# A four-layer graph network on one core: graph matrices kept as 64x64 squares instead of block-diagonal 128x128 tiles, node counts and row sums moved from TensorE to VectorE

## The reference, cut to what matters

```
L0: 8-head attention inside a graph; weights = 0.33*(softmax + adj + exp(-adj)); @ v @ W_out
L1: deg = sum(adj, -1);  agg = (adj / max(deg, eps)) @ x;  relu([x, agg] @ W.T)
L2: H = (adj != 0); w = adj[0, :];  Dn_c = 1 / sum_e H[c,e] w[e];  Be_e = 1 / sum_c H[c,e]
    conv(x, W) = Dn * (H @ (Be * (H.T @ (x @ W.T)))) + b      (1/0 is taken as 0)
    conv(layer_norm(relu(conv(x, W1))), W2) + x
L3: xg = x * sigmoid(deg * Wd + bd);  QK = sigmoid(xg @ Wqk.T + b);  s = (QK @ QK.T) * adj
    attn = s / (sum(s, -1) + eps);  relu(attn @ xg @ Wl.T + bl + xg @ Wr.T)
```

## Time and profile before

| | |
|---|---|
| timed runs, median (range) | 1393.59 us (1392.63 to 1394.86) |
| profiled execution, span from first to last instruction | 1392.5 us |
| PE busy / weight load | 1263.1 us (91%) / 1088.0 us (78%) |
| DVE / ACT / POOL busy | 962.2 us (69%) / 568.9 us (41%) / 505.1 us (36%) |
| mean granted TensorE clock | 0.979 |

### The profile page before, as it was taken

How to read it: one execution, slowest core, us unless ns; L and a number is a source line. 1 busy time by engine, 2 the same in 40 slices (tenths; PEclk the granted TensorE clock), 3 DMA queues, 4 the chain that set the end, 5 groups by cost and what they waited for, 6 DMA issues and landing times.

```text
span 1392.5 us, 30787 instructions
## 1 busy us (share of the span) xinstructions
PE 1263.1 (91%) x11784; PEld 1088.0 (78%) x11784; DVE 962.2 (69%) x2116; ACT 568.9 (41%) x1090; POOL 505.1 (36%) x632
## 2 busy tenths in 40 slices
PE   6789999999999999999999999999999999999776
PEld 4577888788788878878787888778878887888665
DVE  4787766777766677776767776677776667777553
ACT  2354353444435344353434435344443534444121
POOL 2335252442525244262423425243352524435130
PEclk9899999999999999999999999999999999999886
DMA  6000101000010100101010010101001010010000
GB/s 194 20 20 21 35 1 39 15 26 27 19 34 0 38 15 19 34 2 51 0 38 15 19 34 0 38 15 38 15 19 34 0 38 19 0 35 2 20 0 16
DMA packets 43873, 34.93 MB, mean 25 GB/s; under 512 B 19319, under 2 KB 38717, under 8 KB 43838
## 3 DMA queue, kind: packets, MB, share of 16 engines
q1 hardware_dynamic: 43112, 34.04, 7.8%
q10 hardware_dynamic: 726, 0.40, 0.2%
HBM read 26.05 MB, written 8.39 MB: 25 GB/s over the span
## 4 chain that ended last, share of the span: by engine, by line
PE 67%; DVE 20%; issue 8%; ACT 2%; POOL 1%; DMA 1%; DVEq 0%; SPq 0%; POOLq 0%; ACTq 0%
PE bank L879 16%; PE bank L881 15%; PE bank L880 15%; PE bank L1054 5%; DVE x L674 4%; PE bank L998 3%; PE bank L971 3%; DVE stats L663 3%; PE bank L875 2%; PE bank L1112 2%; DVE x L810 1%; DVE yw L821 1%; PE bank L946 1%; DVE hT_lo L604 1%; DVE dsafe L758 1%
## 5 line engine op out<-in xcount | busy, mean ns | idle before, releaser
L407 POOL TENSOR_SCALAR var<-mv 128x2 f32<-128x2 f32 (+1 forms) x192 | 48.0, 250 | 697.3 <-DVE mv L667 697.3
L499 ACT ACTIVATE hT_hi<-bank 128x512 fp32r<-128x512 f32 x160 | 89.6, 599 | 171.0 <-PE bank L998 144.4
L674 DVE TENSOR_SCALAR x<-x,mv,rstd 128x256 f32<-128x256 f32 x256 | 129.6, 553 | 30.0 <-POOL rstd L410 29.9
L410 POOL TENSOR_TENSOR rstd<-var,negh 128x2 f32<-128x2 f32 (+1 forms) x192 | 127.0, 662 | 16.0
L604 DVE TENSOR_TENSOR hT_lo<-bank,hT_hi 128x512 fp32r<-128x512 f32 x160 | 103.7, 683 | 35.3 <-ACT hT_hi L499 30.9
L511 ACT ACTIVATE v<-bank 64x256 f32<-64x256 f32 x256 | 96.8, 378 | 56.6 <-PE bank L881 53.5
L663 DVE BATCH_NORM_STATS2 stats<-x 128x6 f32<-128x256 f32 x256 | 96.4, 418 | 4.4
L516 ACT ACTIVATE prob<-prob 128x512 f32<-128x512 f32 x64 | 40.5, 633 | 127.3 <-DVE prob L708 127.3
L499 ACT ACTIVATE qT<-bank 128x512 f32<-128x512 f32 x64 | 38.3, 598 | 129.0 <-PE bank L881 129.0
L452 POOL TENSOR_TENSOR prob<-prob,srec 128x512 f32<-128x512 f32 x64 | 66.8, 1044 | 52.9 <-DVE srec L716 52.9
L457 POOL TENSOR_TENSOR prob<-prob,mix 128x512 f32<-128x512 f32 x64 | 82.2, 1284 | 6.1 <-POOL prob L452 2.1
(11 more groups left out here) (204 smaller groups left out, 3978.2 us busy)
## 6 DMA issues: line engine op xcount, KB each, us to landing
xTin<-in_x_t SPq DMA_DIRECT2D x32, 256.0 KB, 2.8
xin<-in_x SPq DMA_DIRECT2D x16, 512.0 KB, 3.7
out_x<-x SPq DMA_DIRECT2D x32, 256.0 KB, 2.3
adjA<-in_adj SPq DMA_DIRECT2D x16, 128.0 KB, 2.6
adjB<-in_adj SPq DMA_DIRECT2D x32, 64.0 KB, 3.1
r<-in_wqkv SPq DMA_DIRECT2D x2, 512.0 KB, 8.7
x<-in_wqkv SPq DMA_DIRECT2D x1, 512.0 KB, 10.4
x<-in_w_out SPq DMA_DIRECT2D x1, 512.0 KB, 10.6
```

Of the source, the lines that this page charges most:

```text
L410: pool.tensor_tensor(rstd[layer][:, lo:hi], var[layer][:, lo:hi], negh[:, lo:hi], ALU.pow).then_inc(SEM[f"rstd{n}"], 1)
L499: act.activation(dst, src[:, :], func, **kw).then_inc(SEM[ready], 1)
L674: ins = dve.tensor_scalar(x[:, t, :], x[:, t, :], mv[layer][:, t, 0:1], rstd[layer][:, t:t + 1], ALU.subtract, ALU.mult)
```

## The change

All matrices of a graph become [128, 4, 64]: partitions 0 to 63 hold the square of one graph of the tile, 64 to 127 that of the other. DVE, POOL and ACT work on 256 elements per partition where they worked on 512. On PE

- a gather is 16 matmuls of a 64x128 stationary and a 64x64 moving tile in place of 8 of 128x128; the two graphs of a tile go to two banks, so that one call fills both, at the place of the first (`agg` 0), and nothing is left for the second on PE. ACT and DVE then read a bank as one graph half (strided writes), and the next product waits for both low parts before its first chunk that needs them;
- `sim` is 16 matmuls of 128 rows and 64 columns, `graph_c` 8 of 64x64, `hyper` 4 of 64x64 with 256 moving columns per call (and its two bias matmuls as before);
- the turns `graph_m`, `graph_d` and `turn_s` are 8 matmuls each against a 64x64 identity (two passes) in place of 4 transposes (one pass);
- the turn of `edge` and the count matmuls are gone. A transposed adjacency comes from DRAM (`adj_t`, one DMA of 128 KB per group), adj's first row is spread over 64 partitions by DMA (`wrow`, two DMAs), and DVE makes the turned edges, the count and the weighted row sum.

With `ht` and `cnt` no longer in `FILLS`, the banks of stream B move on: `turn1` 0 now waits for `out3` 1 of the round before to be read (before: for `agg3` 1), `turn1` 1 for `agg3` 0. The core of the diff:

```
-FILLS = {"graph_a": ["ht"], "graph_b": ["cnt"], "graph_c": ["sym"], "graph_m": ["meanT"], "graph_d": ["gT"],
+FILLS = {"graph_a": [], "graph_b": [], "graph_c": ["sym"], "graph_m": ["meanT"], "graph_d": ["gT"],
...
+        adjB = sb("adjB", [P, T, N])
+        adjBt = sb("adjBt", [P, T, N])
+        wrow = sb("wrow", [P, T, N])
+        edgew = sb("edgew", [P, T, N])
...
+        def by_half(ap, h):
+            return ap.rearrange("p c (t h n) -> p h c t n", t=T, h=2)[:, h]
...
+                    sp.wait_ge(*count("dsum", b, 1, 1))
+                    sp.wait_ge(*count("ht_ready", b, 1, 1))
+                    sp.dma_start(adjBt[:, :, :], adj_tg[b]).then_inc(SEM["adjBt_in"], 16)
+                    for h in range(2):
+                        sp.dma_start(wrow[h * N:(h + 1) * N, :, :], adj_w[b, h, 0:1, :, :]
+                                     .broadcast_to([N, T, N])).then_inc(SEM["wrow_in"], 16)
                     sp.wait_ge(*count("meanA_ready", b, 1, 1))
                     sp.wait_ge(*count("sim_ready", b, 1, 1))
+                    sp.dma_start(adjB[:, :, :], adj_g[b]).then_inc(SEM["adjB_in"], 16)
...
+            def halves_out(g, fill, i, dst, ready):
+                act.wait_ge(*filled(fill, i, g))
+                act.activation(by_half(dst, i), bank_of(fill, i)[:, :].rearrange("p (c t n) -> p c t n", c=C, t=T),
+                               ACT.Copy).then_inc(SEM[ready], 1)
+            def low_half(pair, fill, name):
+                def part_of(g, i):
+                    dve.wait_ge(*count(f"{name}_hi", g, i + 1))
+                    dve.tensor_tensor(by_half(pair[1], i), bank_of(fill, i)[:, :].rearrange("p (c t n) -> p c t n", c=C, t=T),
+                                      by_half(pair[0].bitcast(F32), i), ALU.subtract).then_inc(SEM[f"{name}_lo"], 1)
...
+            def flipped(name, g, src):
+                pe.wait_ge(*emptied(name, 0, g))
+                dst = bank_of(name, 0)
+                for t in range(T):
+                    for h in range(2):
+                        ins = pe.matmul(dst[square(h), t * N:(t + 1) * N], src[square(h), t, :],
+                                        ident[square(h), square(h)], start=True, stop=True, skip_group_check=True)
...
+            def gathered(name, g, src, mat, halves=None):
+                for c in range(C):
+                    for t in range(T):
+                        at = slice((c * T + t) * N, (c * T + t + 1) * N)
+                        for h in range(2):
+                            if c == 0 and t == 0:
+                                pe.wait_ge(*emptied(name, h, g))
+                            ins[h] = pe.matmul(bank_of(name, h)[:, at], src[square(h), t, c * P:(c + 1) * P],
+                                               mat[square(h), t, :], start=True, stop=True, skip_group_check=True)
...
-                                 [count("spread_lo", g, c + 1) for c in range(C)]), "up", i)
+                                 [count("spread_lo", g, 2)] * C), "up", i)
```

More of the change, by code:

```diff
@@ L210, in graph_layers @@
         xg = yw
-        sim = hT0
+        pair_s, sim, sT = two("sim")
         smat = sim
-        sT = bhT
+        lend = sb("lend", [P, HID + D + P])
         simsum = sb("simsum", [P, T])
@@ L1068, in mean @@
                           + [(tile_of(aggT, c, t), chunk(wm, C + c)) for c in range(C)],
-                          ready=[count("agg_lo", g, c + 1) for c in range(C)])
+                          ready=[count("agg_lo", g, 2)] * C)
             def spread(g, i):
-                pe.wait_ge(*count("gT_ready", g, 1))
-                gathered("spread", g, i, xl[1], gT, "x2_ready")
+                if i == 0:
+                    pe.wait_ge(*count("gT_ready", g, 1))
+                    gathered("spread", g, xl[1], gT, "x2_ready")
             def up(g, i):
@@ L1108, in simi @@
                 dst = bank_of("sim", 0)
+                apart(pe, g)
                 for t in range(T):
                     for c in range(C):
-                        tile = qkT[:, c, t * P:(t + 1) * P]
-                        ins = pe.matmul(dst[:, t * P:(t + 1) * P], tile, tile, start=(c == 0), stop=(c == C - 1))
+                        for h in range(2):
+                            one = qkT[:, c, t * P + h * N:t * P + (h + 1) * N]
+                            ins = pe.matmul(dst[square(h), t * N:(t + 1) * N], one, one, start=(c == 0),
+                                            stop=(c == C - 1), skip_group_check=True)
                 now_full(ins, "sim", 0)
@@ L1130, in out3 @@
                           + [(tile_of(agg3, c, t), chunk(wlr, c)) for c in range(C)], (HID + D, HID + 2 * D),
-                          [count("agg3_lo", g, c + 1) for c in range(C)])
+                          [count("agg3_lo", g, 2)] * C)
             steps = {
@@ L1136, in _ @@
                 "turn1": lambda g, i: turned("turn1", g, i, xl[0], "x1_ready", 2),
-                "graph_a": graph_a, "graph_b": graph_b, "graph_m": graph_m, "graph_c": graph_c, "graph_d": graph_d, "agg": agg,
+                "graph_m": graph_m, "graph_c": graph_c, "graph_d": graph_d, "agg": agg,
                 "mean": mean, "spread": spread, "up": up,
```

231 lines of the change are left out of this document (95 added, 136 removed).

## The result

The changed kernel takes 1422.69 us (median of 4 runs, 1421.14 to 1423.83) against 1393.11 (4 runs, 1388.42 to 1394.86) for the kernel before on the same chip: a ratio of 1.0219, interval 1.02 to 1.0238. I had forecast 1388. It is 30 us slower, outside my range and on the other side.

What follows compares the result with a forecast made beforehand. Repeated rounds bound the kernel, their head by the chain DVE, POOL, DVE rather than PE's work. Savings of 1.5 + 2.0 + 1.4 = 4.9 us from the profiled 1392.5, with the median 1.1 above, gave 1388; range 1368 to 1397.

Steps and rivals of the forecast that it cites:

- From the end of out3 to mixmat the round runs on the chain DVE, POOL, DVE: Head of each round: claimed that DVE and POOL, not PE's work, bound it; `mixmat` to come 0.94 us earlier.
- That costs nothing as long as DVE's chain is later: `turn1` waits some 0.93 us for DVE's `out3` read under the new bank order; claimed hidden, cost 0.
- The head, 0.94: From `graph_a` to `mixmat`: halved elementwise work on DVE and POOL was to bring `mixmat` 0.94 us earlier.
- From mixmat to up: Costlier `graph_d` and waiting for both low parts leave 0.10 of 0.94 us: 1.5 us over 15 rounds.
- The sim stage, -0.14: `sim` 0.62 us less, `turn_s` and `agg3` 0.24 more each: 0.14 less a round, 2.0 us over 14 rounds.
- for going in and out: 0.23 us per group of tiled PE passes for entering and leaving tiles, taken from `pv`.
- Once: Outside the repeated round: 1.4 us saved by dropping the split of adj's rows; last two rounds 0, new DMAs nothing.
- Low clock: Rival: PE's waits and half-idle array lower its clock in most rounds, 1 to 1.5 us each: +15, 1403; chance 0.05.
- The gather streams: Rival: row tiles hide the gathers' weight loads, `agg3` takes 1.08 us, the kernel 1370; chance 0.27.

## Why the prediction was wrong, step by step

By the ratios, times 1392, the 30.5 us are: 13.5 for the loop (0.0221 less 0.0124), 4.3 for the bank order (0.9998 less 0.9967), 11.6 for the squares (0.9959 less 0.9876) and 1.1, which is not told from nothing, for moving the counts once the squares are there. The intervals leave the four uncertain by some 4, 2.5, 3 and 2 us. The split of the first two depends on the order: with the old banks first it is 1.5 for the banks and 16.3 for the loop.

A round in the written-out kernels, by the rows shown above, with `sim` by its starts on PE's timeline (705.92 and 786.99, 711.36 and 792.79; us):

| from | to | before | changed, old banks | difference | forecast |
|---|---|---|---|---|---|
| `sim` | DVE's last `out3` read | 16.03 | 16.14 | +0.11 | -0.14 |
| that read | `mixmat` | 10.93 | 10.00 | -0.93 | -0.94 |
| `mixmat` | `up` 0 | 15.45 | 16.34 | +0.89 | +0.84 |
| `up` 0 | next `sim` | 38.66 | 38.95 | +0.29 | 0 |
| the round | | 81.07 | 81.43 | +0.36 | -0.24 |

So in a round the stretch with `hyper` and the `sim` stage failed, by 0.29 and 0.25; the two largest terms came as forecast. (The sum of the working, 1393.6 less 4.9, is 1388.7; it was put down as 1388.)

**"From the end of out3 to mixmat the round runs on the chain DVE, POOL, DVE" and the loop's length.** Wrong by omission, and the largest part. Nothing in my working asked how many instructions PE's loop holds. The trace had it: 24 instruction packets for the whole kernel before, so the loop was not refetched, and 104 matmuls with 104 loads added to each round (13448 less 11784, by 16). The runs with idle matmuls show that length brings the refetch and the gap. What I can't settle is the size in the changed kernel: the 13.5 us hold the refetch and whatever else differs between the two kernels' loops. In the profiled executions a round without a stretch of low clock took 83.40 us in the loop and 81.87 written out, before 82.26 and 81.07: 1.53 and 1.19, which is 4 us in 13 rounds. The five rounds of the loop that have such a stretch are together 7 us longer than the others, and the same kernel written out has none. So about half of this share goes with the clock. Whether the stall brings the clock down no run shows; with 200 idle instructions the stall is there in 12 rounds and only two have such a stretch.

**"That costs nothing as long as DVE's chain is later" (the bank wait).** Wrong. I compared PE's arrival at `graph_m` with `meanA` and found slack. But DVE stands in its own order behind `turn1`: the low halves come before `deg`, so `turn1`, ACT's copy and DVE's low half head the very chain that I took as later. Written out it costs 4.3 us (a round is 81.87 with the new banks, 81.44 with the old). In the loop it seems to hide in the gap behind the jump, which would be why restoring the banks there gave nothing that can be told.

**The head, 0.94.** Right: 0.93 from DVE's last `out3` read to `mixmat`. (From `sim` to `mixmat` it is only 0.72 by the chain's rows, because that stretch holds the `sim` stage too.) But the cause is the squares, not the counts. With the squares alone the same stretch takes 9.95 us (726.52 to 736.47), `mixmat` no longer waits at all (in the kernel before written out it waits 0.73), and PE waits 0.89 for `edge`. On PE the counts lay in slack, on VectorE they are on the chain, and only at 256 elements does this come out even.

**"From mixmat to up", 0.10 left.** Right in the sum, by luck: 0.04 is left (0.93 less 0.89). PE waits for the second low part as forecast (0.22 at `up` 0; 4.8 us over 16 in the looped kernel), and `graph_d` cost next to nothing where I had 0.24; but the product of `mean` has become 0.3 slower. First pass of it and first pass of `v`, before written out and squares alone:

```profile
735.08 0.37 PE L879 MATMUL bank<-wm_hi,hT_hi 128*128 128x256 f32 x1
...
740.62 0.40 PE L879 MATMUL bank<-wv_hi,xT_hi 128*128 128x512 f32 x1
```

```profile
738.88 0.38 PE L888 MATMUL bank<-wm_hi,hT_hi 128*128 128x256 f32 x1
...
744.73 0.39 PE L888 MATMUL bank<-wv_hi,xT_hi 128*128 128x512 f32 x1
```

5.54 us against 5.85 for the same 48 passes, and 5.86 with the counts moved as well. It isn't the banks (both have the old order), nor a wait, nor the clock (1.00 in both), nor squares on PE alone: the kernel with the counts alone, all matrices 128x128, took 5.76. Where it comes from stays open.

**The sim stage, -0.14.** Wrong: +0.11. The tile prices were right: `sim` 1.08, a turn 0.61 for 0.41, the gather 1.93 for 1.71. The stage gained nothing, because each return from tiles to full passes costs too. Twelve passes of `q` behind `sim`, before and squares alone:

```profile
707.62 0.48 PE L879 MATMUL bank<-xT_hi,wq_hi 128*128 128x512 f32 x1
...
710.51 0.66 PE L1120 MATMUL bank<-ident,hT 128*128 128x128 f32 x4
```

```profile
711.48 0.50 PE L888 MATMUL bank<-xT_hi,wq_hi 128*128 128x512 f32 x1
...
714.48 0.68 PE L1020 MATMUL bank<-ident,sim 64*64 64x64 f32 x16
```

3.00 for 2.89. My 0.23 "for going in and out" was taken from `pv` and left this out. Behind `turn_s` it is another 0.1, and a third 0.1 behind `agg3`. With the stretch that holds `hyper`, for which I took nothing and named 0.2 as the other end, 0.29 longer, a round of the squares is 0.4 us longer than before where I had it shorter.

**"Once", the last two rounds: 0.** Wrong. The last round costs 4.1 us more in the changed kernel (82.6 from its `sim` to the next, 78.5 before), and 6.5 in the written-out pair (82.9 with the squares, 76.4 before). There no other stream's work lies between, so every latency shows, and PE is at half clock for more of it: the mean granted clock from `sim` to `sim` is 0.73 with the squares and 0.87 before, both written out (0.75 and 0.81 in the loops). How much of the 6.5 is clock and how much waiting no run separates. `up` 0 in the last round of the changed kernel:

```profile
1354.19 1.12 PE L1054 MATMUL bank<-gmat,x 64*128 64x64 f32 x8 [2.46 <-issue]
1355.48 2.83 PE L1054 MATMUL bank<-gmat,x 64*128 64x64 f32 x24 [0.17 <-DVE x L681]
1360.31 0.79 PE L887 MATMUL bank<-w_hi,spT_hi 128*128 128x512 f32 x1 [1.46 <-DVE spT_lo L612]
```

1.46 us for both halves, where the kernel before, ready chunk by chunk, started `up` 0 without a wait (bias at 1332.73, first pass at 1332.80). I had put the halves at 0.6 to 1 for each of four gathers and the savings against them at 2. A gather that fills its banks by chunk, so that `up` could start on the first, wasn't tried.

**Low clock, a rival at 0.05.** It happened in part. Windows of one us over the span show one stretch at 1.2 GHz in the 13 rounds of the loop before, five in the changed kernel and a sixth in the round behind them, five with old banks written out, one with squares alone, none with the new banks written out. The late rounds of 85.34 us are among those with one. The middle of one, in the written-out kernel with old banks:

```profile
656.00:657.00 1.00, 1.00 (x49) 1.00 (x43) 0.90 (x4) 0.00 (x0) 0.00 (x0) 0.50 0.06 16
```

It falls during `score` and the turn of gmat, behind the head's two waits, and such a round is 1.5 us longer (82.9 for 81.4). In the changed kernel five more stretches, at 1.5 us, are some 7 us of the 29 between the two profiled spans, most of them in the loop's share above. No run turned the clock alone, so its share is read, not tested.

**The gather streams, 0.27.** Fell: 1.93 us where I had taken 1.94. The slope of the earlier trace rows as I stated it, 0.9 ns a column, gives 115 ns for 128 columns and 2.07 us; the 0.107 in the working is the time of a full pass. The Trainium skill's rate for loads ("TensorE: Matmul & The Clock Gate", LDWEIGHTS) gave an estimate of 1.94; its factor of up to 2 for a contraction of 64 ("TensorEngine Tiling (Array Packing)", Theoretical Speedup) does not come with 128 weight columns: alternating gained 3.32 to 1.93, which only brings it back near the 1.71 of full passes.

## What to carry to other kernels

Count the instructions that a change adds to the busiest engine's loop: if the instruction queue's packets jump from once through the program to some in each round, the jump back stalls, whatever the added work costs. When you call a wait hidden, follow what stands behind it on every engine, not only when its own engine is needed next. Cut a matrix into squares where the columns to load are halved too (`sim`), not where only the moving side is (the gathers), nor where a transpose of one pass becomes a matmul of two (the turns), and price the return to full passes.

## What the runs showed of the hardware that I had not expected

- A loop of 1632 instructions on TensorE is kept, one of 1732 is fetched again in each round, 135 packets of 16 KB in the whole kernel. The changed kernel's loop (1739) was fetched again at each of three starts; beginning it 95 instructions later gave a second stall of 2.06 us.
- A loop that is not refetched still has a price, jump and register work together: writing it out took 1.2% off the kernel before.
- 64-row passes with 128 weight columns: 104 ns one after another in one row half, 120 ns for a pair in two halves, over groups of 32; starts 112 ns apart in both.
- The same 256-column passes took 5.54 us for 48 in one kernel, 5.76 in another and 5.85 in a third, with no wait between; unexplained.
